# The wait for the transposes moves from ScalarE's copies of mixed y to SyncE's second transfer

## The reference

```python
y = einsum('bct,bcd->bdt', x, cond_w[condition])       # 64 batches of 64 channels, T = 1024
top, sel = top_k(y @ gate_w.T, 2); w_full = scatter(softmax(top), sel)
result = y @ base_w.T + base_b                          # 1024 x 1024
low = y @ lora_A.T                                      # 8 experts of rank 16
out = x + result + 2.0 * sum_e w_full[e] * (low[e] @ lora_B[e].T)
```

## Time and profile before

| | |
|---|---|
| median of 3 runs | 477.48 us (477.19 to 477.62) |
| profiled execution, its time | 478.04 us |
| its span | 476.3 us |
| TensorE (PE) busy | 469.9 us, 99% |
| VectorE (DVE) busy | 351.2 us, 74% |
| ScalarE (ACT) busy | 159.5 us, 33% |
| GpSimd (POOL) busy | 117.0 us, 25% |
| granted TensorE clock | full speed in all 40 slices |
| DMA | 76.91 MB, 161 GB/s on average |

### The profile page before, as it was taken

One profiled execution on the slowest core, in us unless ns is written; L12 is line 12 of the kernel. 1 busy time (PEld: TensorE's weight loads), 2 busy tenths in 40 slices (PEclk: granted clock), 3 DMA queues, 4 the chain that ended last, 5 costly groups with the idle time before them and its releaser, 6 DMA issues.

```text
span 476.3 us, 8144 instructions
## 1 busy us (share of the span) xinstructions
PE 469.9 (99%) x2660; PEld 460.7 (97%) x2660; DVE 351.2 (74%) x636; ACT 159.5 (33%) x262; POOL 117.0 (25%) x113
## 2 busy tenths in 40 slices
PE   8999999989999999999999999999999999999997
PEld 8999999989999999999999999999999999999996
DVE  4867979897686867869587686867869587585843
ACT  5734444223332422333223332322333223432300
POOL 2344241041420414123041420414114041310400
PEclk9999999999999999999999999999999999999999
DMA  8976633626355262743625356262643626343202
GB/s 314 411 226 223 194 95 132 217 72 223 112 183 194 96 227 54 246 128 132 220 88 199 110 179 195 88 221 65 231 144 133 212 87 210 112 170 120 89 22 88
DMA packets 49275, 76.91 MB, mean 161 GB/s; under 512 B 13666, under 2 KB 32226, under 8 KB 49250
## 3 DMA queue, kind: packets, MB, share of 16 engines
q1 hardware_dynamic: 37586, 71.88, 43.5%
q10 hardware_dynamic: 11664, 4.72, 3.8%
HBM read 41.98 MB, written 34.60 MB: 161 GB/s over the span
## 4 chain that ended last, share of the span: by engine, by line
PE 97%; DMA 1%; issue 0%; DVE 0%; ACT 0%; SPq 0%
PE acc L907 50%; PE acc L899 29%; PE acc L945 10%; PE mixed L939 9%; DMA x_sb<-in_x_first 1%; PE acc L925 0%; PE mixed L925 0%; DVE y_lo L611 0%; ACT y_hi L464 0%; DVE x_sb L892 0%; SPq L285 0%
## 5 line engine op out<-in xcount | busy, mean ns | idle before, releaser
L386 POOL TENSOR_TENSOR x_sb<-x_sb,bias 128x1024 f32<-128x1024 f32 x32 | 76.9, 2422 | 221.4 <-DVE x_sb L744 198.2
L899 PE MATMUL acc<-r_hi,y_lo 128*128 128x392 f32 x256 | 87.0, 340 | 0.2 <-DVE y_lo L611 0.2
L899 PE MATMUL acc<-r_hi,y_hi 128*128 128x392 f32 x256 | 86.9, 339 | 0.0
L899 PE MATMUL acc<-r_lo,y_hi 128*128 128x392 f32 x256 | 86.6, 339 | 0.0
L907 PE MATMUL acc<-t_hi,s_hi 128*128 128x384 f32 x224 | 74.9, 334 | 1.4 <-issue 1.4
L907 PE MATMUL acc<-t_lo,s_hi 128*128 128x384 f32 x224 | 74.9, 334 | 0.0
L907 PE MATMUL acc<-t_hi,s_lo 128*128 128x384 f32 x224 | 74.8, 334 | 0.0
L907 PE MATMUL acc<-t_lo,y_hi 128*128 128x384 f32 x216 | 72.4, 335 | 0.0
L907 PE MATMUL acc<-t_hi,y_lo 128*128 128x384 f32 x216 | 72.3, 335 | 0.0
L907 PE MATMUL acc<-t_hi,y_hi 128*128 128x384 f32 x216 | 72.2, 334 | 0.0
L652 DVE TENSOR_TENSOR y_lo<-y_turned,y_hi 128x512 fp32r<-128x512 f32 x60 | 45.2, 793 | 25.6 <-ACT y_hi L520 25.4
(11 more groups left out here) (81 smaller groups left out, 741.5 us busy)
## 6 DMA issues: line engine op xcount, KB each, us to landing
x_sb<-in_x SPq DMA_DIRECT2D x32, 512.0 KB, 4.7
out<-x_sb SPq DMA_DIRECT2D x31, 512.0 KB, 3.1
y_scratch<-y_whole SPq DMA_DIRECT2D x60, 256.0 KB, 2.1
y_moved<-y_scratch SPq DMA_DIRECT2D x120, 128.0 KB, 2.8
t_raw<-in_w_quads SPq DMA_DIRECT2D x4, 768.0 KB, 10.0
scratch<-low_turns ACTq DMA_DIRECT2D x16, 128.0 KB, 1.7
low_turns<-scratch ACTq DMA_DIRECT2D x64, 32.0 KB, 2.3
r_raw<-in_w_plain SPq DMA_DIRECT2D x8, 196.0 KB, 5.3
```

Source lines behind the costliest of these rows:

```text
L386: nc.gpsimd.tensor_tensor(x_sb[:, slot(c), :], x_sb[:, slot(c), :], bias[:, :], ALU.add) \
L899: return nc.tensor.matmul(acc[:, i, 0:NP], y_part[:, i, k, :], w_part[:, k, :], start=(k == 0 and product == 0), stop=(k == KT - 1 and pro ...
```

## The change

In `y_copy` ScalarE no longer waits for `turned`: a copy needs its mix (`mix_done`) and the earlier store out of the same half of `y_whole` (`y_out`). In `move` SyncE now waits once for both copies and then issues the first store; ahead of the second store it waits for `turned` of the pair before. The loads into `y_moved` follow the second store on the same engine, and so still come after the transposes that read the tile's old contents.

```diff
--- before.py
+++ after.py
@@ -309,8 +309,11 @@
             def move(j, u, i):
 
                 s = 3 * j + u
+                sp.wait_ge(y_copied, 4 * s + 2 * i + 2)
                 for h in range(2):
-                    sp.wait_ge(y_copied, 4 * s + 2 * i + h + 1)
+                    if h == 1 and (u > 0 or i > 0):
+
+                        sp.wait_ge(turned, 4 * s + 2 * i)
                     half = slice(h * (T // 2), (h + 1) * (T // 2))
                     sp.dma_start(y_scratch[i, :, half], y_whole[:, half]).then_inc(y_out[h], 16)
                 for q in range(QUARTERS):
@@ -480,8 +483,6 @@
                     if u > 0 or i > 0:
 
                         act.wait_ge(y_out[h], 16 * (2 * s + i))
-
-                        act.wait_ge(turned, 4 * s + 2 * i)
                     nc.scalar.copy(y_whole[:, h * (T // 2):(h + 1) * (T // 2)], mixed[:, h, :]).then_inc(y_copied, 1)
 
             def gate_exp(j, u):
```

## The result

The changed kernel is slower: a median of 478.89 us (10 runs, 478.05 to 480.79) against 477.55 us (10 runs, 477.19 to 477.87), a ratio of 1.0027 with a 95% interval of 1.0017 to 1.0037. That is 1.34 us more, where the forecast was 1.04 us less. Its times also spread more widely. Three executions that took from 1,205 to 1,912 us, one of e10, one of e12 and one of the kernel before beside them, stand in no median, range or ratio of this document.

The account below looks back on a forecast made before the run. TensorE, 99% busy, bounds the kernel; its one gap, in step 2, would shrink by 1.04 us, taking the profiled 478.04 to 477.0 and the median 477.48 to 476.4. Likeliest case 475.9 to 476.8; 8 in 10 from 475.7 to 477.2.

Parts of the forecast that it names:

- What bounds the kernel, and where the change acts: TensorE is 99% busy; step 2 costs 1.59 us more than its work, every loop step nothing.
- every loop step stays at 28.7 us: Sign of being right: loop steps, where TensorE is busy throughout, keep their time.
- the gap: TensorE in step 2, before S1 x T1: starts at 97.39, 1.52 us late, 0.10 after VectorE's `take` 2.
- The copies, the issue and VectorE's way: Step 2: copies can run by about 88.4, transfer issued at 88.70, `y_low` without its 1.29 us wait.
- Rival 2: ScalarE's transfer issue in step 2 is not set free and stays at 90.48; time 477.4 to 477.5; chance 0.13.
- The later first store: SyncE's first store waits for the second copy, about 0.47 us; cost taken as nothing, bounds 0.27 earlier and 0.47 later.
- ScalarE's way: Step 2: transfer issued at 88.70 lands 2.5 us later, at 91.20; TensorE starts at 96.35, 1.04 us sooner.
- the sign of being wrong: ScalarE's low-value transfer in step 2 landing later than 3.5 us.
- The row of step 0: The same transfer issued in step 0 among stores took 2.7 us, used as the loaded end, giving 0.84 us gain.
- the sum as written: Step 2 chain from landing: four issues 1.78 us, `x_high`, `x_low`, `take` end 2.09 later, TensorE 0.10 after.
- the 2.85 us: Landing estimate for step 2's transfer if engines alternate between queues packet by packet; gain 0.7 us.
- Rival 4: Slower: a straggling DMA engine makes step 2's transfer land 4.5 us after issue; time 478.4; chance 0.07.

Follow-up runs that it names:

- e10: The changed kernel with, in step 2, VectorE's `take` 2 ahead of `x_low` and GpSimd's bias additions waiting for `lowT_low`: 478.94 us, ratio 1.0014.
- e12: The changed kernel with GpSimd's bias additions in step 2 also waiting for `lowT_low`, VectorE's order unchanged: 478.43 us, ratio 1.0010.
- e11: The kernel before with, in step 2, `take` 2 ahead of `x_low` and GpSimd's additions waiting for `lowT_low`: 476.70 us, ratio 0.9972.
- e13: The changed kernel with, in step 2, the second x load later, `take` 2 ahead of `x_low` and GpSimd waiting for `lowT_low`: 476.60 us, ratio 0.9965.
- e14: The kernel before with, in step 2, the second x load later, `take` 2 ahead of `x_low` and GpSimd waiting for `lowT_low`: 476.66 us, ratio 0.9969.
- e6: The changed kernel with SyncE issuing the second x load behind the move of pair 1 in step 2: 477.66 us, ratio 0.9999 to the kernel before.
- e15: The changed kernel with step 2's second x load later and, in all steps, SyncE's first store held until the transposes end: 476.78 us, ratio 0.9970.
- e9: SyncE's part of the change alone, ScalarE's copies waiting for the transposes as in the kernel before: 477.66 us, ratio 1.0003.
- e7: The changed kernel itself timed and profiled again: 479.23 us over 4 runs, ratio 1.0035 to the kernel before.
- e5: The kernel before with VectorE running `take` 2 ahead of `x_low` in step 2: 477.43 us, ratio 0.9998.
- e4: The changed kernel with VectorE running `take` 2 ahead of `x_low` in step 2: 479.37 us, ratio 1.0044, in two groups.
- e2: The changed kernel with ScalarE's queue in step 2 waiting for pair 0's transposes ahead of the low-value transfer: 480.37 us, ratio 1.0059.
- e3: The changed kernel with ScalarE in step 2 casting x ahead of the four transfers back: 478.99 us, ratio 1.0023, in two groups.

## Why the prediction was wrong

**What bounds the kernel, and where the change acts: right in the main.** Nearly all of the difference lies in step 2 (in e10 in step 3 too, and step 3 is 0.3 to 0.5 us longer in e11, e13 and e14), and the loop steps from step 5 on stay at 28.7 us in every profile. The sign "every loop step stays at 28.7 us" did not hold for step 4, which takes 28.85 and 28.82 in the two profiles of the change. That the gap hangs on the `take` behind `x_low` was borne out by e10, which took it from there and closed the gap with a landing as late as the change's; that it hangs on ScalarE's transfer by e6 and e15, which closed it by an earlier landing.

**The copies, the issue and VectorE's way: right.** Copies from 87.34 to 88.6 (forecast by 88.4), issue at 88.61 (88.70), `y_low` without its wait. Rival 2, that the issue is not set free, fell. The later first store (SyncE, e9) cost nothing by itself, as forecast.

**The step that failed** is "ScalarE's way": "I take 2.5, nearer the loaded row, since the loads last for only some of its flight. It lands at 91.20". It landed after 4.07 and 4.72 us, later than the 3.5 that the prediction had named as the sign of being wrong. The row of step 0 was not a bound: there 0.5 MB of stores shared the engines with the transfer, here 1 MB of loads stood ahead of it and the stores were beside it. With 4.72 from 88.61 the sum as written gives `x_high` done at 96.26 and TensorE at 98.5, which is what the trace has, 98.46. So the mechanism was right and the term was mis-sized, by enough to turn the sign. I had also worked out that the first store leaves for the engines at 88.4, "behind the x loads", and gave it no price there; e15 against e6 and e13 shows 0.4 to 0.6 us, with one load ahead. The page DMA: Bandwidth & Descriptors of the Trainium skill, section on queues, rings and completion order, has the engines alternate between queues, and the 2.85 us that I had worked out from it was short as well. The fault was in my reading. I let the turn change with every row of 4 KB, but the section says that an engine drains a whole packet from one queue first, and it counts a packet as 9 to 17 descriptors typically and 64 at most. The packets that the profile counts here are single rows, and an x load has 128 of them, eight to an engine if they are shared evenly. So by the page a whole load, or two, can go ahead of the transfer in one turn. The rows agree with that as far as they go: of the 256 rows of the loads all but 20 had started when the transfer's first did, at 91.15. No run shows how rows are grouped. The sum itself does not come out either: rows 7 give 0.17 us for a row of 4 KB on one engine, eight of them 1.35, and so a landing at 3.1 and not 2.85.

**What was left out** is the way behind the gap. I followed the transfer to `x_high` only; the low values that it carries also come back later, `lowT_low` falls behind the start of GpSimd's addition, and stands for 2.2 us more. In the profile of e7 it holds TensorE for 0.60 us in step 2; in the kernel before with the `take` first it is what stands between e5 and e11, 0.9 us, each taken against the kernel before on its chip; and e10, rid of it, has no group above 480 as e4 had. It has no term in the prediction, though the trace of before shows an instance.

**Rival 4** named the outcome, slower by about 1 us through a landing 4.5 us after the issue, with a chance of 0.07. It gave the wrong reason, one straggling engine, where all 16 were busy with loads; that the early store adds to it was right. The range of 8 in 10 ended at 477.2, below even the unchanged time, because the landing was taken as nearly sure to come within 2.7 us, the row of step 0, in which the transfer had stores beside it and not 1 MB of loads ahead. Nor did the prediction see that the x loads do not leave at a fixed time: SyncE's first store leaves 0.15 us later in the step with the change (80.79 less 72.36, against 80.36 less 72.08), and when it lands moves everything behind.

**Not settled**: what lets the clock fall. It fell behind the 2.15 us stop in the first profile and the 2.57 us stop of e2, and not behind the 2.21 us stop of e12. It is in two of the ten runs of the change (mean clock 0.995, the two longest, 479.94 and 480.79), so it is not what makes the median. Three executions of the kernel before, beside e10 to e15, have it too (0.995 and 0.996, at 480.22 to 481.20), so the change does not bring it in; whether it makes it more frequent is not shown. Nor is it shown why a transfer waits for the other queue's loads; only that it does: its first packet comes 0.85 us after the issue in the trace of before and 1.36 to 2.63 us after it in the seven profiles of an early issue behind two loads. What splits e3 and e4 into two groups is open but for the hint in the rows of e4.

## What to carry to other kernels

An earlier issue is not an earlier landing: before a transfer is moved ahead, list what other queues will have in flight at its new time, ahead of it and beside it, in MB, and price the landing by when those are through. When an engine's late operation is mended or shifted, follow its data to every reader, and look at which operations of VectorE and GpSimd it brings to overlap, since a 0.4 us operation can cost 2.6 behind a long one. In a kernel with one gap the gap itself is the cheaper target: a reordering on VectorE and one wait of GpSimd (e11), with the copies' wait left as it was, gave 1.0 us, and the change with the same gap closed (e13) gave no more than the kernel before so mended (e14).

## What the hardware showed that I had not expected

- A transfer of 0.13 MB on ScalarE's queue moved no packet for 2.4 us while SyncE's queue, issued 1.9 us earlier, kept 16 engines busy with 1 MB of loads; its time to landing went from 1.76 to between 2.25 and 4.73 us with what stood ahead, how long that had been under way, and what stood beside.
- VectorE's `lowT_low`, 128 x 256 elements with two SBUF inputs, took 0.42 us, and 1.67 to 2.64 us in step 2 when it met a GpSimd addition of 128 x 1024 already running: it ended 0.3 us after the addition, whenever it had come.
- After a stop of 2.15 us TensorE's granted clock stood at 0.50 for about 3 us, from 99.5 to 102.5; after one of 2.57 us (e2) it was at 0.50 from 99 to 102, and after one of 2.21 us in a third kernel (e12) it stayed at 1.00.
